# Attention over eight batches: group statistics with a PSUM operand, begun half a batch ahead, in two parts

## What is computed

```python
xg = x.reshape(B, 32, C // 32, N)                    # 32 groups of 8 channels
xn = (xg - mean(xg)) * rsqrt(var(xg) + 1e-5)         # over channels of the group and positions
xn = xn * scale + bias
# layer 2: 8 heads of 32 channels, softmax over the 1024 positions
weight = softmax(q^T k * 32 ** -0.5)                 # 1024 x 1024 for each head
out = x + w_proj @ (weight v) + b_proj
# layer 3: group norm again, then attention over the 8 heads of one position
attn = softmax(einsum('bnhd,bngd->bnhg', q, k) * 32 ** -0.5)
out = x + proj(einsum('bnhg,bngd->bnhd', attn, v))
```

## Time and profile before

| | us |
|---|---|
| median of three runs | 2064.46 |
| lowest and highest | 2063.97, 2068.48 |
| profiled execution | 2065.67 |
| its span, first to last instruction | 2063.7 |
| PE busy | 1820.6 (88%) |
| DVE busy | 1485.6 (72%) |
| POOL busy | 1189.5 (58%) |
| ACT busy | 786.5 (38%) |

### The profile page before, as it was taken

The page is one execution under the profiler, slowest core; times in us unless marked ns, Lnnn a source line. Parts: engine busy times, 40 slices in busy tenths (PEclk is TensorE's granted clock), DMA queues, the critical chain, the costliest instruction groups (busy, mean ns, idle before and its releaser), DMA issues.

```text
span 2063.7 us, 37560 instructions
## 1 busy us (share of the span) xinstructions
PE 1820.6 (88%) x15416; PEld 811.3 (39%) x15416; DVE 1485.6 (72%) x2203; ACT 786.5 (38%) x1546; POOL 1189.5 (58%) x509
## 2 busy tenths in 40 slices
PE   5987876879999999999999999999999868888884
PEld 2332322334444433433443443434443444554541
DVE  5666657787776777777777777787776148888875
ACT  0441220014454554553544544544545323333320
POOL 0471210016586675756756666567676238888896
PEclk8898888879999999999999999999999989999996
DMA  5000011030000101001001001001001121222121
GB/s 175 1 2 0 1 48 73 0 123 27 22 2 5 59 1 43 22 2 62 2 2 63 2 2 63 2 1 62 2 2 42 42 68 28 87 74 84 48 70 43
DMA packets 48160, 75.10 MB, mean 36 GB/s; under 512 B 30532, under 2 KB 30838, under 8 KB 47990
## 3 DMA queue, kind: packets, MB, share of 16 engines
q1 hardware_dynamic: 38486, 72.11, 9.9%
q10 hardware_dynamic: 9504, 0.59, 0.3%
HBM read 44.83 MB, written 25.17 MB: 34 GB/s over the span
## 4 chain that ended last, share of the span: by engine, by line
PE 72%; DVE 18%; issue 3%; ACT 3%; DMA 2%; POOL 1%; POOLq 0%; SPq 0%; DVEq 0%; ACTq 0%
PE AV L641 13%; PE S L615 6%; DVE MX L1249 4%; PE S L592 3%; PE RB L861 3%; PE S L678 3%; PE RB L615 3%; PE S L627 2%; PE AV L874 2%; PE S L652 2%; PE S L619 2%; DVE ENC L1600 2%; PE S L750 2%; PE RB L910 2%; DVE BN L1283 2%
## 5 line engine op out<-in xcount | busy, mean ns | idle before, releaser
L1158 POOL TENSOR_TENSOR ACC<-ACC,PR 128x1024 f32<-128x1024 f32 x288 | 671.9, 2370 | 98.4 <-ACT PR L995 98.3
L1249 DVE TENSOR_REDUCE MX<-S 128x1 f32<-128x512 f32 x644 | 410.0, 683 | 150.0 <-PE RB L592 70.8
L995 ACT ACTIVATE PR<-S 128x512 f32<-128x512 f32 x678 | 363.6, 604 | 385.8 <-PE S L627 230.7
L1158 POOL TENSOR_TENSOR ACC<-PR 128x1024 f32<-128x1024 f32 x72 | 168.9, 2368 | 554.3 <-ACT PR L995 554.3
L641 PE MATMUL AV<-PR,VT 128*32 128x512 f32 x2304 | 317.2, 623 | 2.5 <-ACT PR L995 2.3
L1249 DVE TENSOR_REDUCE MX<-RB 128x1 f32<-128x512 f32 x345 | 224.4, 683 | 76.4 <-PE S L592 62.2
L995 ACT ACTIVATE PR<-RB 128x512 f32<-128x512 f32 x312 | 175.0, 604 | 208.4 <-PE S L627 118.8
L615 PE MATMUL S<-HI 32*128 32x512 f32 x678 | 202.1, 496 | 19.9 <-DVE MX L1249 13.8
L1184 POOL TENSOR_TENSOR PR<-WO,WRK 128x1792 f32<-128x1792 f32 x32 | 155.7, 4878 | 32.9 <-DVE ENC L1600 14.9
L1184 POOL TENSOR_TENSOR PR<-WO,VT 128x1792 f32<-128x1792 f32 x32 | 154.8, 4851 | 23.7 <-DVE ENC L1600 13.8
L592 PE MATMUL S<-HI 32*128 32x512 f32 x644 | 159.8, 510 | 6.0 <-ACT PR L995 3.3
(11 more groups left out here) (314 smaller groups left out, 3477.7 us busy)
## 6 DMA issues: line engine op xcount, KB each, us to landing
X<-out_y SPq DMA_DIRECT2D x24, 1024.0 KB, 5.0
out_y<-X SPq DMA_DIRECT2D x16, 1024.0 KB, 4.9
X<-in_x SPq DMA_DIRECT2D x8, 1024.0 KB, 8.6
OHU<-out_y SPq DMA_DIRECT2D x8, 512.0 KB, 4.4
X<-out_y SPq DMA_DIRECT2D x8, 512.0 KB, 4.1
out_y<-X SPq DMA_DIRECT2D x8, 512.0 KB, 3.1
out_y<-OHU SPq DMA_DIRECT2D x8, 512.0 KB, 3.1
WO<-WO SPq DMA_DIRECT2D x128, 16.0 KB, 1.8
```

The costliest lines, as they stand in the source:

```text
L995: nc.scalar.activation(exps(s, pair)[:, HALF * one:HALF * one + HALF], RING[ring.place()], ACT.Exp, scale=1.0 if i is None else float(D) * ...
L1158: nc.gpsimd.tensor_tensor(ACC[:, pair, :], so_far, exps(s, pair), ALU.add).then_inc(pool_used, 1)
L1249: nc.vector.tensor_reduce(out=MX[:, h, t, keys:keys + 1], in_=bank(), op=ALU.max, axis=AX.X).then_inc(ring_free, 1)
```

## The change

1. `group_stats(0)` no longer has operations on two SBUF operands. It reads the means from the PSUM bank in two subtractions: one writes DEV to SBUF, the other writes into the bank. The product and the final sum then have one operand from the bank each. That is one operation more, and the bank is given back after the last one.
2. The statistics come in two parts, one for each channel tile, at two consecutive steps, and `gn 0` follows at the third.
3. In iterations 0 to 6 the odd window does this for batch `i + 2`, at steps 11, 12 and 13. In iteration 0 the even window does it also for batch 1, at steps 8, 9 and 10. `gn 1` and `norm_apply` stay at step 12 of the even window; in the last iteration `gn 1` and POOL's factors for layer 3 stand there too, and its odd window has no group norm.
4. Since `gn` is now true in the last even window too, its four `v` jobs stand at steps 7, 9, 9 and 10 as in the others, instead of 4, 6, 7 and 10.

```diff
-def window_jobs(post=False, nxt=True, gn=False, trail=True, single=False):
+def window_jobs(post=False, nxt=True, gn=False, ahead=0, trail=True, single=False):
...
+    if ahead:
+        first = MT + 3 if ahead == 2 else MT
+        jobs[first].append(("stats", 0, ahead))
+        jobs[first + 1].append(("stats", 1, ahead))
+        jobs[first + 2].append(("gn", 0, ahead))
     if gn:
-        jobs[MT].append(("stats",))
-        jobs[MT + 2].append(("gn", 0))
-        jobs[MT + 4].append(("gn", 1))
+        jobs[MT + 4].append(("gn", 1, 1))
...
-            window(u, 0, window_jobs(post=not first, gn=not last, trail=not first), i)
-
-            window(u + 1, 1, window_jobs(nxt=not last, gn=last), i)
+            window(u, 0, window_jobs(post=not first, gn=True, ahead=int(first), trail=not first), i)
+
+            window(u + 1, 1, window_jobs(nxt=not last, ahead=0 if last else 2), i)
...
-                    if jobs and ("gn", 1) in jobs[s]:
-                        if par == 0:
+                    if jobs and ("gn", 1, 1) in jobs[s]:
+                        if i < B - 1:
                             norm_apply(i + 1)
...
-            def statistics(batch):
+            def statistics(batch, parts=(0, 1)):
                 wait(dve, xin_in, 16 * (batch + 1))
-                src = XIN if not isinstance(batch, int) or batch <= B else xn3(batch - B)
-                for t in range(CT):
+                src = XIN if batch <= B else xn3(batch - B)
+                for t in parts:
                     for half in range(2):
                         last = nc.vector.bn_stats(BN6[:, t, half, :], src[:, t, HALF * half:HALF * half + HALF])
                 link(last)
-                link(nc.vector.bn_aggr(MV[:, 0, :], BN6[:, 0]))
-                link(nc.vector.bn_aggr(MV[:, 1, :], BN6[:, 1]))
-                dve.sem_inc(gn_ready, 1)
+                for t in parts:
+                    last = nc.vector.bn_aggr(MV[:, t, :], BN6[:, t])
+                link(last)
+                if 1 in parts:
+                    dve.sem_inc(gn_ready, 1)
 
             def group_stats(k, batch):
                 src = bank()
                 if k == 0:
-                    nc.vector.tensor_copy(MG[:, :], src[:, 0:CT]).then_inc(ring_free, 1)
+                    mean, dev, square = src[:, 0:CT], src[:, CT:2 * CT], src[:, 2 * CT:3 * CT]
+                    nc.vector.tensor_copy(MG[:, :], mean)
+                    nc.vector.tensor_tensor(DEV[:, :], mean, MV[:, :, 0], ALU.subtract)
+                    link(nc.vector.tensor_tensor(dev, mean, MV[:, :, 0], ALU.subtract))
+                    link(nc.vector.tensor_tensor(square, dev, DEV[:, :], ALU.mult))
+                    nc.vector.tensor_tensor(S2[:, :], square, MV[:, :, 1], ALU.add).then_inc(ring_free, 1)
                     own()
-                    link(nc.vector.tensor_tensor(DEV[:, :], MV[:, :, 0], MG[:, :], ALU.subtract))
-                    link(nc.vector.tensor_tensor(S2[:, :], DEV[:, :], DEV[:, :], ALU.mult))
-                    link(nc.vector.tensor_tensor(S2[:, :], S2[:, :], MV[:, :, 1], ALU.add))
                     dve.sem_inc(gn_ready, 1)
```

More of the change, by code:

```diff
@@ L732, in window @@
                         elif job[0] == "gn":
-                            group_sums(job[1], i + 1)
+                            group_sums(job[1], i + job[2])
                         elif job[0] == "post":
@@ L1337, in window @@
                         elif job[0] == "stats":
-                            statistics(i + 1)
+                            statistics(i + job[2], (job[1],))
                         elif job[0] == "gn":
-                            group_stats(job[1], i + 1)
+                            group_stats(job[1], i + job[2])
                         elif job[0] == "post":
```

## The result

The changed kernel takes 1999.41 us (median of four runs, 1997.5 to 2000.47) where the kernel before takes 2065.7 beside it (four runs): a ratio of 0.9677, 95% interval 0.966 to 0.9694. The profiled execution took 2000.47 us with a span of 1998.5. The forecast was 2000 with 1987 to 2023.

What follows compares the result with a forecast made beforehand. PE's order of work was taken to wait for DVE, whose two-SBUF-operand operations wait for POOL. 48.5 + 8.5 - 12.6 + 0.5 + 20 = 65 us gained, from 2065.67 to about 2000 us; 8-in-10 range 1987 to 2023.

Steps and rivals of the forecast that it cites:

- The hold, and operands from PSUM: DVE group: operations with two SBUF operands wait for POOL; with PSUM operands, five cost 1.2 us with waits (0.8 to 2).
- Even windows: Second halves in iterations 1 to 6 lose statistics and gn 0 and fall to 35.8 us, gaining 48.5 us.
- Iteration 0: Even window's second half keeps its statistics, in two parts; gain 8.5 us (6.8 to 9.8).
- Odd windows: Iterations 0 to 6: statistics cost 1.3 us and gn 0 0.6; 1.8 a window (1.0 to 3.5), 12.6 in seven.
- The rival that they pay in full, with the clock: Odd windows use no idle time and suffer a clock drop: 5.2 us instead of 1.8, total 2024 us; chance 0.15.
- The argument against it: Odd windows: each part meets its own idle time; the clock fell after a 2.98 us pause, none that size due.
- The last iteration: Odd window gains 1.6 us from POOL's dropped factors, even window 0.4 worse; net gain 0.5 us (-1 to 2).
- L3: Layer 3: the half batch with statistics falls from 25.64 to about 21.5 us; 20 us gained in all (16 to 22).
- I take 4.0 a batch, five times: Layer 3: each of five batches gains 4.0 us where the DVE and POOL bounds meet, 20 us together.
- half of the L3 gain is eaten: Rival: DVE, POOL or an unseen third chain (PE's products, ACT's copies) binds layer 3; 10 us less, 2010 us; chance 0.12.
- The held-anyway rival: One SBUF operand suffices to wait for POOL: four operations wait 2.3 us each; 36 us slower, 2101 us; chance 0.04.
- the new wait in even windows: Rival: POOL or another engine binds earlier in even windows; half of 48.5 us stays, 2024 us; chance 0.04.

Runs made afterwards that it cites:

- the pair with one operation more: Changed kernel plus one unused 128x2 DVE operation behind the group: with two SBUF operands 2028.09 us (0.9791), with a PSUM operand 1995.38 us (0.9639).
- the variant in one part: Changed kernel with the statistics in one lump, at step 12 of odd windows and step 8 of iteration 0's even window: 2019.31 us, ratio 0.9768 to the kernel before.
- The extra SBUF operation: Changed kernel with one more 128x2 DVE operation behind the group, two SBUF operands, result unused: 2028.09 us, ratio 0.9791 to the kernel before.

## Why the prediction was right

**The hold, and operands from PSUM: right.** The row of 432 ns was the right one to read it from; 80 operations of 138 to 168 ns and the pair with one operation more show it. The group takes 0.70 us, 0.92 to 0.94 in L3 with the wait behind it (DVE has work waiting there), and not 1.2: operations without a semaphore between them start 0.07 us apart, so the fifth was nearly free. The price of a PSUM operand doesn't show: 150 for DEV, 159 for S2, 160 shortest for DEV before. By the Trainium skill (VectorE: DVE Perf Modes, the section on the TRN2 errata) some 65 ns more would have been due for each, an estimate from its table; the rows of this case don't have them.

**Even windows: right to 0.5 us in 49.** Halves of 35.7 where I said 35.8, and the idle time did take the two `v` products. Iteration 0: 36.42 and 8.4 instead of 8.5.

**Odd windows: right, sum and terms.** The two parts of the statistics cost 0.56 and 0.69 (said 1.3 together), gn 0 0.6 (said 0.6), in all 1.85 a window (said 1.8). The rival that they pay in full, with the clock, didn't come, but the variant in one part shows how near it was: 0.34 us lie between the end of the second part and PE's product. The argument against it, no pause of the size of 2.98 us, was the wrong one. What kept the clock at 1.00 in these rows is only that PE's longest pause is 0.34 us. A row of my own spoke against the argument: the half of 40.67 has PEclk 0.92, no hold, and this as PE's longest pause.

```profile
639.76 0.50 PE L615 MATMUL S<-HI 32*128 32x512 f32 x1 [0.45 <-DVE MX L1249]
642.25 1.94 PE L641 MATMUL AV<-PR,VT 128*32 128x512 f32 x8
```

**The last iteration: right in sum (0.8 against 0.5), wrong in the parts.** The even window didn't get 0.4 worse but 0.5 better: the first half gave back 1.8 and the second took 1.3. The odd one is POOL's, as said. Its last eight steps fall from 28.7 to 21.5 us, and then PE waits:

```profile
1565.96 1.94 PE L660 MATMUL SUM<-ACC,ONES 128*32 128x512 f32 x8 [5.26 <-POOL ACC L1161]
```

It restarts at the 1.2 GHz level (1.94 for eight matmuls that took 1.04 before), and 0.3 us are left of 7.2.

**L3: the total right, its terms wrong.** The step that failed is "I take 4.0 a batch, five times". An undisturbed batch gains 5.3: 4.5 in the half with statistics, as 25.64 to 21.14, and 0.85 in the other. I had costed only the half in which DVE is held, and from a base that doesn't fit: the 20.13 of rows 11 is a half of the last batches, while the halves without statistics between the held ones took 22.15. Both bounds that I had worked out, 21.5 and 21.6, lie above the 21.14 that was measured. In the other one PE waited for ACT and ran at PEclk 0.92:

```profile
1743.06 2.45 PE L861 MATMUL RB<-X 128*32 128x256 f32 x32 [3.86 <-ACT WRK L1057]
```

After, its longest wait for ACT at this place is 1.0 us. The extra SBUF operation brings the 0.85 back in three of the five halves, and in all five a wait for ACT of 2.6 to 3.9 us at this place, so it belongs to the hold; through what ACT is late I have not followed. Five batches would give 26.8. Against that stand the pause in PE's issue with what follows (the half of 25.34 instead of 21.14: 4.2, and 1 in the next) and 2.0 at the first batch, where DVE waits 8.27 us for the load of XIN instead of 6.46. None of these was in the sum. The rival "half of the L3 gain is eaten" had something in it, then: 7.2 of 26.8 us were, by the pause and the load and not by a third chain, and a gain that I hadn't seen paid for it. That 20 came out is partly luck.

**The held-anyway rival and the new wait in even windows** have nothing for them: no 128x2 row above 168 ns, PE busy 35.64 of 35.69 us.

## What to carry to other kernels

Look for a short DVE operation whose longest duration is many times its shortest at one shape, and compare it with POOL's row of the same time: with two SBUF operands it waits for POOL's running operation, and giving it one operand from PSUM was worth more here (3.0%) than moving it (0.6%). Where a job has to be added to a PE-bound step, split it so that PE never has to stand still for it: a pause of 0.96 us cost 1.5 to 4.1 us more through the clock in six windows of seven, and one of 0.46 us 1.2 to 1.5 in three of seven. And when a stage gets faster, look at what its DMAs now meet; here PE stood still for 2.3 us twice while a store was under way, and with the store in another place the half of the first pause was 3.1 us shorter, at the price of 2.3 to 2.6 in another.

## What I had not expected

- A hold ends with one of POOL's operations, nearly always the running one: at the end of POOL's row the third operation took 0.16 us (874.66 against 874.61). Once it lasted over two (4.01 us from 724.36 on). How many of a row of held operations pay is a matter of phase, and small shifts elsewhere change it.
- A hold in one half batch costs time in the next one too, 0.85 us.
- PE stood still in its issue for 2.3 us in the middle of 128 small matmuls, and most of that went when a store of 1 MB (two of 512 KB) was issued at another time.
- PE's granted clock fell after a pause of 0.96 us in six windows and did not in a seventh with the same program; after 0.45 and 0.46 us it fell in four halves.
